# A perceiver block on one NeuronCore: GpSimd makes the diagonals of the spreading product between the two late context differences instead of behind both

## The reference, cut to what matters

```
x = x + cross_attention(layernorm(x), ctx)   # 16 heads of 32, rotary angles on q and k
x = x + causal_self_attention(layernorm(x))
x = x + mixture_of_8_experts(layernorm(x))   # top 2 of 8
```

## Time and profile before

| what | value |
|---|---|
| median of 3 runs | 777.29 us (777.06 to 777.75) |
| the profiled execution: its own time | 776.16 us |
| its span, first to last instruction | 774.3 us |
| mean granted TensorE clock | 0.986 |
| first layer's loop, about | 50 to 530 us of the span |

### The profile page before, as it was taken

One profiled execution on the slowest core, in us unless ns is written; L12 is line 12 of the kernel. 1 busy time (PEld: TensorE's weight loads), 2 busy tenths in 40 slices (PEclk: granted clock), 3 DMA queues, 4 the chain that ended last, 5 costly groups with the idle time before them and its releaser, 6 DMA issues. The chain is left out here.

```text
span 774.3 us, 23209 instructions
## 1 busy us (share of the span) xinstructions
PE 739.7 (96%) x9494; PEld 646.1 (83%) x9495; DVE 560.2 (72%) x1293; ACT 408.4 (53%) x930; POOL 345.6 (45%) x364
## 2 busy tenths in 40 slices
PE   8999999999999999999999999997899999599997
PEld 7888889999899989988989989985677777478884
DVE  6786786967868768778697696755888998812236
ACT  5445466565566556555656556553566665133330
POOL 1664455456456545655545545521132221246640
PEclk9999999999999999999999999999999999789999
DMA  8310301121101011010120110133943238634538
GB/s 287 142 35 23 118 2 58 64 69 58 38 28 56 9 57 58 9 56 6 54 64 2 57 64 2 57 110 109 366 195 136 96 124 321 219 124 172 183 130 325
DMA packets 23317, 78.99 MB, mean 102 GB/s; under 512 B 3344, under 2 KB 4752, under 8 KB 20144
## 3 DMA queue, kind: packets, MB, share of 16 engines
q1 hardware_dynamic: 19536, 65.50, 23.6%
q0 software_dynamic: 3680, 12.06, 4.7%
HBM read 58.93 MB, written 18.61 MB: 100 GB/s over the span
## 5 line engine op out<-in xcount | busy, mean ns | idle before, releaser
L1356 PE MATMUL bank<-ctx_parts_hi,wparts 128*128 128x258 f32 x224 | 67.2, 300 | 0.7 <-DVE ctx_parts_lo L890 0.7
L890 DVE TENSOR_TENSOR ctx_parts_lo<-craw,ctx_parts_hi 128x1032 fp32r<-128x1032 f32 (+1 forms) x56 | 63.2, 1129 | 2.7 <-ACT ctx_parts_hi L626 2.6
L1357 PE MATMUL bank<-ctx_parts_hi,wparts 128*128 128x258 f32 x224 | 63.3, 283 | 0.0
L1358 PE MATMUL bank<-ctx_parts_lo,wparts 128*128 128x258 f32 x224 | 63.3, 282 | 0.0
L1383 PE MATMUL bank<-wparts,ctx_parts_hi 128*128 128x256 f32 x224 | 63.1, 282 | 0.0
L1381 PE MATMUL bank<-wparts,ctx_parts_hi 128*128 128x256 f32 x224 | 62.9, 281 | 0.0
L1384 PE MATMUL bank<-wparts,ctx_parts_lo 128*128 128x256 f32 x224 | 62.9, 281 | 0.0
L657 ACT ACTIVATE v<-bank 128x512 f32<-128x512 f32 x56 | 33.2, 594 | 52.8 <-PE bank L1384 52.3
L475 POOL TENSOR_TENSOR ksin<-kb_even,const 128x258 f32<-128x258 f32 (+1 forms) x42 | 46.7, 1112 | 31.5 <-ACT kb_even L647 30.2
L661 ACT ACTIVATE wraw<-wraw,nmax 128x257 f32<-128x257 f32 x96 | 47.9, 501 | 22.8 <-DVE nmax L983 21.0
L1356 PE MATMUL bank<-ctx_parts_hi,w_sums_hi 128*128 128x258 f32 x168 | 52.0, 309 | 0.6 <-DVE wraw L962 0.4
(11 more groups left out here) (413 smaller groups left out, 2623.6 us busy)
## 6 DMA issues: line engine op xcount, KB each, us to landing
craw<-ctx_t_dram SPq DMA_DIRECT2D x32, 516.0 KB, 4.3
expert_lo<-weights_dram SPq DMA_DIRECT2D x8, 1024.0 KB, 12.2
expert_hi_scratch<-wraw SPq DMA_DIRECT2D x16, 512.0 KB, 2.6
wparts<-expert_hi_scratch SPq DMA_DIRECT2D x8, 1024.0 KB, 8.9
wraw<-weights_dram SPq DMA_DIRECT2D x6, 1024.0 KB, 4.9
expert_lo<-ffn_out_scratch SPq DMA_DIRECT2D x16, 256.0 KB, 5.5
x<-x_dram SPq DMA_DIRECT2D x8, 256.0 KB, 4.4
craw<-weights_dram SPq DMA_DIRECT2D x2, 1024.0 KB, 5.0
```

Source lines behind the costliest of these rows:

```text
L890: dve.tensor_tensor(dst[1], src, dst[0].bitcast(F32), ALU.subtract).then_inc(s_clo, 1)
L1356: pe.matmul(psum, whi_i[:, i, cols], hi[:, i, :], start=own and i == 0, stop=False, skip_group_check=not own)
L1357: pe.matmul(psum, wlo_i[:, i, cols], hi[:, i, :], start=False, stop=False, skip_group_check=not own)
L1358: last = pe.matmul(psum, whi_i[:, i, cols], lo[:, i, :], start=False, stop=i == 1, skip_group_check=not own)
```

## The change

In the even batches from 4 to 28 POOL makes the two diagonals between T2 and T4; before, it made them behind T4. Batch 2, which goes through the plain branch, and batch 30, which has no next pair, keep their order. No instruction is added or removed.

```diff
-                def ctx_sums_late(q):
+                def ctx_sum_t2(q):
                     pool.wait_ge(s_clo, parts_of(q, O_22))
                     pool.wait_ge(s_tr, ctx_sum_of(q, R_T3))
                     pool.tensor_tensor(craw[1][:, 2:4, :], craw[1][:, 2:4, :], t1_raw, ALU.subtract).then_inc(s_tr, 1)
+
+                def ctx_sum_t4(q):
                     pool.wait_ge(s_tr, ctx_sum_of(q, R_T2))
                     pool.tensor_tensor(craw[0][:, 2:4, :], craw[0][:, 2:4, :], craw[1][:, 2:4, :], ALU.subtract).then_inc(s_tr, 1)
...
                         if b == PLAIN - 2:
-                            ctx_sums_late(q)
+                            ctx_sum_t2(q)
+                            ctx_sum_t4(q)
...
                         for i in range(3):
                             k_sin(b + 1, i)
                         if q <= PAIR_LAST:
-                            ctx_sums_late(q)
+                            ctx_sum_t2(q)
                         diagonals(b)
+                        if q <= PAIR_LAST:
+                            ctx_sum_t4(q)
                         ln_and_bias(t, j)
```

## The result

The changed kernel's median is 774.79 us over 10 runs, against 776.82 for the kernel before over 10 runs. The ratio is 0.9964 with a 95% interval of 0.9949 to 0.9980: faster by 0.36%. (The two medians by themselves give 0.9974, 2.0 us; that lies within the interval.) On the 777.29 us from which the prediction started this gives 774.5 us, 2.8 us less (interval 1.6 to 4.0); I had said 1.6 us less, with 774.6 us as the low end.

What follows compares the result with a forecast made beforehand. PE, busy 96% of the span, was taken to bound the kernel. Four batches at 0.65 us together and two at 0.96 us gave 1.61 us less than 777.29, so 775.7 us, range 774.6 to 777.1.

Steps and rivals of the forecast that it cites:

- The stall and its price: PE's spreading product waits for the second diagonal in six j = 2 batches; 0.48 us each, 2.9 us at the most.
- The turns of DVE and POOL: Their instructions with SBUF inputs exclude each other; in batch 10 the diagonals would end at 204.98 and 205.74, T4 at 208.00.
- T4's room: In batch 10 T4 may end by 208.18 without delaying ACT's rounding; 0.18 us to spare, so cost 0.
- What PE keeps in batches 6, 10, 18 and 22: PE arrives sooner but is stopped at k_product(q, 1, 5) by DVE's k_sum; 0.16 us kept each, 0.65 us in all.
- DVE's gapless order: In batch 11 DVE works without a gap from O_T4's low part into the masking, so the k_sum does not come earlier.
- Batches 14 and 26: DVE idles 0.73 and 1.07 us ahead of the next masking, so the whole 0.48 us stays in each; 0.96 us.
- a sign of being wrong: The prediction is wrong if, among other signs, PE's lost time within the scores moves or vanishes.
- The batches with j = 0: The spreading product does not wait there, and T4 1.4 us later is still early; no gain or cost was counted.
- the one that capped batches 14 and 26: Rival: these two batches give no more than the others; 6 x 0.16 = 1.0 us, 776.3 us, chance 0.16.
- the open question: Whether what PE waits for within the scores behind batches 14 and 26 comes at a fixed time; "issue" names no releaser.
- Full recovery: Rival: all six stalls come back as gain, DVE's chain moving with PE; 2.9 us, 774.4 us, chance 0.12.

Runs made afterwards that it cites:

- after_trig_late: The changed kernel with DVE's two q_trig products moved from the end of the j = 2 batches to just ahead of the next batch's q_rotate; ratio 0.9920 to the kernel before.
- t4_late: The changed kernel with one more small POOL instruction between the diagonals and T4 in the j = 2 batches; ratio 0.9998 to the kernel before.
- only_j0: The kernel before with the diagonals between T2 and T4 only in the j = 0 batches (4, 8, 12 to 28); ratio 0.9985 to it.
- only_14_26: The kernel before with the diagonals between T2 and T4 in batches 14 and 26 only; ratio 0.9978 to it.

## Why the prediction was wrong

- **The stall and its price**: right. 0.48 us at the spreading product, six times, gone with the earlier diagonals; the table shows 0.36 us ahead of the product, and the 0.11 behind it once the `k_sum` no longer stops PE (11.10 us before, 10.99 in after_trig_late).
- **The turns of DVE and POOL**: right to 0.01 us for both diagonals and for T4 in batch 10; in the other five batches with j = 2 they fall alike.
- **T4's room**: right, 0.17 us measured against 0.18, and t4_late shows what lies beyond it.
- **What PE keeps in batches 6, 10, 18 and 22**: 0.16 us said, 0.22 measured (and 4 x 0.16 is 0.64, not 0.65). The mechanism, the masking behind DVE's gapless order, is the one that after_trig_late takes away.
- **Batches 14 and 26**: the step that failed. I took PE's lost time within the scores as given, let the whole 0.48 us stay because DVE idled behind it, and expected that idle time to remain. The forecast had named it as a sign of being wrong that this lost time moves or vanishes; it vanished. It hung on the very wait that the change removes. With it gone DVE no longer idles, PE meets the `k_sum` wait there too, and the direct gain is 0.22 us as elsewhere; but 0.80 and 1.07 us of lost time go. Instead of 0.96 us these two batches gave 2.3.
- **The batches with j = 0**: costed at nothing, as PE waits for no diagonal there. That term had no reason of its own beyond the missing wait. They gave 0.54 and 0.17 us, by the same path as far as the runs tell: only_j0 shows both go, but only_14_26 loses the 0.54 too with batch 20's order unchanged.
- **The rivals**: the one that capped batches 14 and 26 assumed that the lost time "comes at a fixed time"; the open question I had named there was the right one, but I had left out the third answer, that it shrinks. Full recovery gave nearly the measured time, 774.4 us, but that is luck: its mechanism is wrong, since DVE's chain did not move with PE.

In sum: 1.3 us direct, 1.6 said; 2.6 us of lost time, 0 said; 3.9 us in the traces. The ratio's 2.8 us (1.6 to 4.0) hold that, near their upper end; the spans of the two profiled executions differ by 3.3 us.

## What to carry to other kernels

A wait can have two prices: what the engine stands, and what its instruction queue, which meets the wait earlier, cannot do meanwhile. Idle time put down to "issue" a few microseconds behind a semaphore wait may be a part of that wait's bill; a trace without the wait tells. And when a stall is removed, look at once for the chain that had been just fast enough because of it: here two DVE products moved by one batch were worth nothing that the ratio could show before the change, and 1.5 us of the loop behind it.

## What the runs showed that I had not expected

- A block of code fetched 1.3 us behind the spreading product cost PE up to 1.2 us in the sine half of the next scores; fetched ahead of it, none. Not every late fetch cost: in batches 16 and 28 of before one stood 1.4 us behind the product and nothing was lost. Moving the program by 64 PE instructions took the three losses out of the order of before (1.8 us) with all of its waits in place.
- PE's instruction queue meets a wait ahead of the engine: in batch 20 of before the second diagonal was ready 0.66 us before its product started, without a wait of the engine, and the fetch behind it still came sooner when the diagonal did: in only_j0 0.7 us ahead of the product, against 1.0 us behind it in the trace of before.
- Sixteen idle matmuls of 256 columns (32 in the trace) ahead of the first product are not hidden by the transfers: the first product starts 6.4 us later.
